# Who issues the bulk transfers of a pass: SP at its seventh place, or ScalarE at the end of its tenth

## The reference, cut to what matters

```python
xn = _layernorm(x, axis=-1)
x = x + _L0_gnn_ref(xn, edge_index, ...) + _L0_mix_ref(xn[None], ...)[0]
x = x + _L0_ffn_ref(_layernorm(x, axis=-1)[None], ...)[0]
...
# in _L0_ffn_ref
top_vals, top_idx = jax.lax.top_k(logits, K)          # K = 2 of E = 8
w = jax.nn.softmax(top_vals, axis=-1)
...
for e in range(E):
    h = jax.nn.gelu(jnp.einsum('bsd,dh->bsh', xn, W1[e]) + b1[e], approximate=False)
    y_e = jnp.einsum('bsh,hd->bsd', h, W2[e]) + b2[e]
    y = y + y_e * w_full[..., e, None]
```

## Time and profile before

| what | value |
|---|---|
| median of 3 runs | 3450.45 us (3449.42 to 3454.7) |
| the profiled execution's own time | 3450.09 us |
| its span, first to last instruction | 3448.4 us |
| PE busy | 2790.3 us, 81% of the span |
| DVE busy | 2317.2 us, 67% |
| POOL busy | 2153.7 us, 62% |
| ACT busy | 1283.3 us, 37% |
| the stage of the change | from about 2262 us to the end |

### The profile page before, as it was taken

The page is one execution under the profiler, slowest core; times in us unless marked ns, Lnnn a source line. Parts: engine busy times, 40 slices in busy tenths (PEclk is TensorE's granted clock), DMA queues, the critical chain, the costliest instruction groups (busy, mean ns, idle before and its releaser), DMA issues. The chain is left out here.

```text
span 3448.4 us, 69443 instructions
## 1 busy us (share of the span) xinstructions
PE 2790.3 (81%) x17326; PEld 2273.5 (66%) x17327; DVE 2317.2 (67%) x6448; ACT 1283.3 (37%) x4258; POOL 2153.7 (62%) x2115
## 2 busy tenths in 40 slices
PE   6858888888899988888888888845348798999998
PEld 4635666666676765666666666635247787999997
DVE  6656666666666666777777777788887676555554
ACT  5713333333333333333333333345445552333332
POOL 3167777777777777666676666705656576444444
PEclk9979999999999999999999999965569899999999
DMA  7646666666666657666666566646667776444443
GB/s 255 247 122 155 159 156 161 158 161 162 162 163 162 164 153 187 180 180 179 179 181 175 168 173 172 166 127 206 222 198 193 219 196 152 73 69 72 71 71 53
DMA packets 400457, 552.06 MB, mean 160 GB/s; under 512 B 64948, under 2 KB 332935, under 8 KB 399994
## 3 DMA queue, kind: packets, MB, share of 16 engines
q0 software_dynamic: 114496, 265.49, 32.9%
q1 hardware_dynamic: 200888, 205.86, 20.4%
q10 hardware_dynamic: 84770, 77.19, 7.0%
HBM read 416.82 MB, written 132.72 MB: 159 GB/s over the span
## 5 line engine op out<-in xcount | busy, mean ns | idle before, releaser
L1142 POOL DMA_INDIRECT rows<-node_rows,index x1552 | 1477.3, 952 | 562.3 <-issue 452.2
L1420 PE MATMUL ps_sum<-msg,hot 128*128 128x260 f32 x3904 | 1014.9, 405 | 18.9 <-DVE big L1239 2.9
L1420 PEld LDWEIGHTS ps_sum<-msg,hot 128*128 128x128 f32 x3904 | 726.7, 196 | 134.4 <-issue 7.7
L1222 DVE TENSOR_TENSOR msg<-rows,ps_w 128x1024 f32<-128x1024 f32 x488 | 595.8, 1221 | 37.2 <-ACT ps_w L1314 21.7
L1926 POOL DMA_INDIRECT out_dram<-big x204 | 359.6, 1763 | 358.2 <-DVE big L2192 261.6
L2066 PEld LDWEIGHTS x_ps_hT<-wq,x_w_ring 128*128 128x128 f32 x3264 | 403.3, 195 | 40.4 <-DVE x_w_ring L2159 24.0
L1986 ACT ACTIVATE wq<-x_ps_hT,x_b1T 128x128 f32<-128x128 f32 x816 | 232.9, 368 | 527.3 <-PE x_ps_hT L2066 527.2
L2066 PE MATMUL x_ps_hT<-wq,x_w_ring 128*128 128x128 f32 x3264 | 406.4, 279 | 26.5 <-DVE x_w_ring L2159 21.7
L1198 DVE TENSOR_SCALAR hotT<-targets,pair_node_id 128x512 bf16 x488 | 189.5, 388 | 348.3 <-SPq L1104 345.9
L1400 PE MATMUL ps_hot<-ident_h,hotT 128*128 128x128 bf16 x1952 | 194.2, 223 | 263.4 <-DVE hotT L1198 260.6
L1915 POOL DMA_INDIRECT expert_in<-f_rows,f_slot x196 | 251.4, 1283 | 206.5 <-DVE f_rows L2326 136.5
(11 more groups left out here) (304 smaller groups left out, 4302.8 us busy)
## 6 DMA issues: line engine op xcount, KB each, us to landing
targets<-dst_row SPq DMA_DIRECT2D x391, 128.0 KB
big<-expert_in SPq DMA_DIRECT2D x204, 130.0 KB, 2.1
rows<-node_rows,index POOLq DMA_INDIRECT x1564
x_w_ring<-in_L_ffn_W_dram SPq DMA_DIRECT2D x42, 512.0 KB, 5.1
node_rows<-big SPq DMA_DIRECT2D x14, 924.0 KB
turned<-rT SPq DMA_DIRECT2D x14, 896.0 KB, 4.6
area<-turned ACTq DMA_DIRECT2D x98, 128.0 KB
queries<-area ACTq DMA_DIRECT2D x98, 128.0 KB
```

Source lines behind the costliest of these rows:

```text
L1142: g.indirect_dma_start(rows[:, j, k, :], None, s.node_rows, bass.IndirectOffsetOnAxis(ap=index[:, b, j * G + k:j * G + k + 1], axis=0)).th ...
L1222: v.tensor_tensor(m[:, :, 0:D].rearrange("p g (h f) -> p g h f", h=GH), rows[:, bass.ds(here, 1), :, 0:D].rearrange("p j g (h f) -> p (j g ...
L1420: mm = pe.matmul(ps_sum[:, j % 2, 0:SUM], hot[:, j % MSGS, k * P:(k + 1) * P], msg[:, j % MSGS, k, :], start=(k == 0), stop=(k == G - 1))
```

## The change

The part at SP's place 7 is taken out, and the same four calls, with the same waits and transfers, stand in ACT's stream after all else that ACT has at place 10. `load_xn` and `load_hx` also stay on SP for the chunks loaded ahead of the rounds. Everything else is unchanged.

```diff
@@ SP @@
                         for it in TILES_AT[n, p]:
                             ahead(it)
-                        if p == 7 and n <= CHUNKS + 1:
-                            if n >= 2:
-                                settle_homes(n - 1)
-                            if n <= CHUNKS:
-                                store(n - 1)
-                            if n < CHUNKS:
-                                load_hx(n)
-                            if n + 1 < CHUNKS:
-                                load_xn(n + 1)
                         if p == 10 and n <= 3:
@@ ACT @@
+                def load_xn(c):
+                    if c >= 2:
+                        act.wait_ge(joined, c - 1)
+                    act.dma_start(xn[:, c % 2, :, :], s.residual[...]).then_inc(xn_loaded[c % 2], 16)
...
+                def settle_homes(freed):
...
+                    act.wait_ge(stored, 16 * freed)
+                    act.wait_ge(measured, freed)
+                    act.wait_ge(rows_ready, freed * CHUNK)
...
                         if p == 10 and 2 <= n < CHUNKS + 2:
                             odds_of(n - 2)
                         first_tiles([look_up, gelu], [0, 2], n, p)
+                        if p == 10 and 1 <= n <= CHUNKS + 1:
+                            if n >= 2:
+                                settle_homes(n - 1)
+                            if n <= CHUNKS:
+                                store(n - 1)
+                            if n < CHUNKS:
+                                load_hx(n)
+                            if n + 1 < CHUNKS:
+                                load_xn(n + 1)
```

More of the change, by code:

```diff
@@ L1762, in load_hx @@
                         sp.dma_start(x_row[0:TAIL, CHUNK - 1, :], x[N - TAIL:N, :]).then_inc(last_loaded, 16)
[L1764 to L1768, removed]
                 def load_fold(e):
@@ L1773, in load_fold @@
                     sp.dma_start(w_ring[:, e % 2, 0:C * HID].rearrange("p (c n) -> p c n", c=C), W1[e].rearrange("(c p) n -> p c n", p=P)).then_inc(fold_in[e % 2], 16)
[L1775 to L1786, removed]
                 def quad_expert_now(q):
@@ L1988, in gelu, with load_hx, store @@
                     ins.then_inc(act_ready, 1)
+                def load_xn(c):
+                    if c >= 2:
+                        act.wait_ge(joined, c - 1)
+                    act.dma_start(xn[:, c % 2, :, :], s.residual[c * CHUNK * P:(c + 1) * CHUNK * P, :].rearrange("(t p) d -> p t d", p=P))\
+                      .then_inc(xn_loaded[c % 2], 16)
+                def load_hx(c):
+                    full = min((c + 1) * CHUNK, TILES - 1) - c * CHUNK
+                    if c >= 1:
+                        act.wait_ge(joined, c)
+                    act.dma_start(hh[:, :, :], s.mixed[c * CHUNK * P:(c + 1) * CHUNK * P, :].rearrange("(t p) d -> p t d", p=P)).then_inc(hx_loaded, 16)
+                    act.dma_start(x_row[:, 0:full, :], x[c * CHUNK * P:(c * CHUNK + full) * P, :].rearrange("(t p) d -> p t d", p=P)).then_inc(hx_loaded, 16)
+                    if c == CHUNKS - 1:
+                        act.dma_start(x_row[0:TAIL, CHUNK - 1, :], x[N - TAIL:N, :]).then_inc(last_loaded, 16)
+                def store(c):
+                    full = min((c + 1) * CHUNK, TILES - 1)
+                    act.wait_ge(joined, c + 1)
+                    act.dma_start(out[c * CHUNK * P:full * P, :].rearrange("(t p) d -> p t d", p=P),
+                                 s.sums[:, c * CHUNK:full, 0:D]).then_inc(stored, 16)
+                def settle_homes(freed):
+                    homes_now = [e for e in range(EXPERTS) if -(-(RINGS + (e + 1) * W_HOME) // (CHUNK * ROW)) == freed]
+                    if freed != -(-RINGS // (CHUNK * ROW)) and not homes_now:
+                        return
+                    act.wait_ge(stored, 16 * freed)
+                    act.wait_ge(measured, freed)
+                    act.wait_ge(rows_ready, freed * CHUNK)
+                    if not homes_now:
+                        act.dma_start(b2_b.rearrange("p e d -> p (e d)"), b2.rearrange("e d -> (e d)").partition_broadcast(P)).then_inc(b2_in, 16)
+                    for e in homes_now:
+                        act.dma_start(w1[:, e, :].rearrange("p (c n) -> p c n", c=C), W1[e].rearrange("(c p) n -> p c n", p=P)).then_inc(experts_in, 16)
+                        act.dma_start(w2[:, e, :].rearrange("p (c n) -> p c n", c=HC), W2[e].rearrange("(c p) n -> p c n", p=P)).then_inc(experts_in, 16)
                 act.wait_ge(mix_root_in, 1)
```

## The result

The changed kernel takes 3544.35 us (median of 4, 3537.88 to 3555.36) against 3450.86 us for the kernel before on the same chip: ratio 1.0272, 95% interval 1.0245 to 1.0300. It is slower, as forecast, and the time lies in the range; it is 11 us above the forecast of 3533.

The account below looks back on a forecast made before the run. It took the pass as bound by the loop from `joined` through the burst to DVE's wait for `f_xn`, delays passing one for one into PE's full tail. 3450.09 + 54.2 (early rounds) + 28.8 (rounds 9 to 13) = 3533 us, range 3488 to 3565.

Parts of the forecast that it names:

- ACT's stream is held by an unmet wait: At the end of ACT's place 10, transfers cannot pass an activation still waiting; issue in round 7 is 6.52 us later.
- the rival built on it: Transfers overtake ACT's waiting activations and go out at `joined`; no early loss, 3423 to 3437 us, chance 0.04.
- 6.52 us per early round: Issue in rounds 2 to 7 comes 6.52 us later each, with nothing hiding it: 39.1 us.
- The shifts: Later issue alone in the early rounds: 39.1 us for rounds 2 to 7 and 3.5 for round 1, 42.6 together.
- The homes with the burst: Rounds 5 to 7: biases and experts' weights start together with the burst, 2.9 us each, 8.7 in all.
- `load_fold` beside the burst: Rounds 2 and 3: SP's load_fold runs beside the burst, 0 to 2.9 us each; half taken, 2.9.
- `xn(9)` hidden with 0.8 us to spare: Issued in round 8: 24.5 us to landing against DVE's use 25.3 us after `joined`, so no cost.
- Rounds 9 to 13: Late rounds, gelu also ahead of the transfers: 20.8 us for later issue plus 8 for sharing, 28.8, bounds 9.5 to 47.6.
- The first step: Round 9: the transfers stand behind the gelu, so `xn(10)` lands late; 12.6 to 15.1 us of new wait on DVE.
- my two bounds: Late rounds: issue when the gelu's product is there, 2.3 us before the odds start, or after the gelu, 2.7 after.
- The sharing with tile loads: Rounds 10 to 13: tile loads run beside the burst, up to 3.9 us each; half taken, 8 us.
- the rival of the longer hold: Issuing holds ACT more than about 13 us, delaying its rows to PE in four rounds; 3567 us, chance 0.09.

Follow-up runs that it names:

- e4: Changed kernel with the four calls at the head of ACT's place 10 instead of its end; 3459.05 us, ratio 1.0014 to the kernel before.
- e8: Changed kernel with settle_homes (biases, experts' weights) left on SP at place 7; 3521.54 us, ratio 1.0203 to the kernel before.
- e9: Changed kernel with load_fold issued by ACT behind load_xn instead of by SP; 3545.24 us, ratio 1.0265 to the kernel before.
- e3: Kernel before with SP waiting for gap_ready ahead of its four calls at place 7 from round 2 on; 3502.64 us, ratio 1.0141.
- e1: Changed kernel with ACT issuing the four calls only in rounds 1 to 8, SP at place 7 after that; 3516.30 us, ratio 1.0176 to the kernel before.
- e7: Kernel before with 14 idle activations more at the end of ACT's place 10 in rounds 10 to 13; 3457.56 us, ratio 1.0016.
- e6: Changed kernel with the calls on ACT in the order load_xn, load_hx, settle_homes, store; 3441.95 us, ratio 0.9972 to the kernel before.
- e5: Kernel before with SP's calls at place 7 in the order load_xn, load_hx, settle_homes, store; 3434.64 us, ratio 0.9948.
- e12: Kernel before with load_xn, then load_hx at SP's place 7, and settle_homes and store at SP's place 10; 3427.00 us, ratio 0.9912.

## Why the prediction was right, step by step

- **ACT's stream is held by an unmet wait** (from the earlier trace rows): right. In every round from 2 on the first transfer leaves with the odds or after them, never at `joined`. This is the step on which the sign hung. The rule of the Trainium skill, page "Advanced Engine Details and Errata", section "Sequencer and Instruction Queues", agrees with this trace only for activations that carry no wait (e4, eight passed); the rival built on it, 3423 to 3437, is out.
- **6.52 us per early round**: right, 6.56 in round 7. The shifts alone were set at 42.6 us (39.1 and 3.5 for round 1); taking the 11.3 that e8 shows for the homes, the 7.2 that e9 shows for `load_fold` and the 0.8 of `xn(9)` (below) from the 59.5 leaves 40.2. A burst with nothing beside it took 13.6 us from odds to L2221 (2416.99 to 2430.63, rounds 4 to 5), a little less than the 15.1 of the earlier trace rows.
- **The homes with the burst**: too small, 8.7 taken, 11.3 measured in the rounds 5 to 7 (e8). The bursts with them take 17.5 to 19.0 us, 3.4 to 4.1 more than the same bursts in e8, where 1.05 MB at 363 GB/s gave 2.9. The rate was taken too high: 363 GB/s is all that moved in the 3 us of the earlier trace rows, and 0.17 of those 1.09 MB were POOL's, which leaves about 306 GB/s for the burst. From issue to use, start included, its own 3.67 MB took 13.6 to 15.1 us, 244 to 269 GB/s. By these paces an estimate for 1.05 MB is 3.4 to 4.3 us.
- **`load_fold` beside the burst**: too small, and outside its own bounds of 0 to 5.8. 2.9 taken, 7.2 measured, 3.6 in each of the two bursts (e9). It needs both the second queue and the later burst: with the later burst in SP's one queue the two take 15.1 and 13.8 us (e3) instead of 18.5 and 17.3, and with ACT's queue on time nothing is lost (e4). Halving what could mix in was the larger error, the rate of 363 GB/s the smaller.
- **`xn(9)` hidden with 0.8 us to spare**: missed by as little; L2221 waited 0.85 us there.
- **Rounds 9 to 13**: 28.8 set, 33.2 measured up to the last join. The first step was 12.1 us (12.6 to 15.1 set). The issue fell 1.6 us behind the start of the odds (2880.43 against 2878.82, and alike in rounds 10 to 12), between my two bounds. It comes 0.08 us behind the start of the gelu's first activation (2880.35), with the load of the gelu's table ahead of that. The product that this gelu waits for was there by 2876.50, so the lower bound, an issue as soon as the product is there, was wrong. Whether the table or the gelu's own wait, long met, holds the transfer is not separated by any run.
- **The sharing with tile loads**: 8 set. From the first issue to the use it takes 20.6, 23.4, 19.3 and 21.6 us in rounds 10 to 13, against 18.8, 17.2 and 18.9 in rounds 10, 12 and 13 before (round 11's is taken against round 10's): 1.8 + 4.6 + 2.1 + 2.7 = 11.2. It lies midway between the half that I took and the 15.6 of everything mixed in. I read it as sharing. e4, which has the tile loads in the other queue too, takes 20.0 to 24.7 us in these rounds, and e1, e3 and e7, with the late burst in SP's queue, 17.1 to 21.1 in the rounds 10, 12 and 13. But the same round differs by one to three us among runs that issue it alike, and no run took the tile loads alone out, so sharing as the cause is argued and not shown.
- **PE**: the wait for expert rows nearly vanished, as forecast. What took its place are ACT's rows and not DVE's copies. That this had no price of its own up to 8.85 us of hold is shown by e7; the rival of the longer hold put that point at 13 us, and ACT was held for 10.0 to 13.6, so in round 13 that point was reached, and its price there is open.
- **The sum**: 54.2 + 28.8 = 83 set, 59.5 + 33.2 - 0.7 = 92 measured. The mechanism and its places held. Early, the homes (+2.6), `load_fold` (+4.3) and `xn(9)` (+0.8) came out above their terms and the shifts (-2.4) below; late, the longer burst came out above. That errors of both signs partly cancelled in the early sum is luck, though a small one.

What the prediction did not see is why a late issue costs at all. It took `f_xn` at the end of the burst as given; e6 shows that with `f_xn` in front the same late issue costs 7 to 14 us against e5 instead of 92, and that the kernel is then even faster than the one before.

## What to carry to other kernels

A transfer issued by a computing engine leaves when that engine's stream reaches it: look for the last activation ahead of it that waits for a semaphore, and put the issue ahead of that one or leave it to an engine whose stream has no such wait there. An engine that only issues can be late as well, as SP is behind the tile loads. Before moving a burst, look at its order: what is waited for goes first, what nobody waits for (a store) last. Here that alone turned 2.7% slower into 0.3% faster (e6), and on SP, with the store and the homes three places later, it made the kernel 0.9% faster than before (e12). And a wait that grows on an engine off the path, 8 to 41 us on PE in e7, is no loss until the time says so.

## What was not expected of the hardware

- How far ACT's stream runs ahead: a transfer went out past eight activations that carry no wait, 3.6 us before the last of them started (e4), but in the late rounds it came only with the start of the gelu, behind the load of its table and 1.6 us behind the odds.
- In these rows issuing held the engine longer when more was queued: the `f_x_row` issue took 1.4 us in round 2 of the changed kernel, 3.5 us in round 7 with weights ahead of it and 8.2 us in round 13 beside tile loads, and ACT did nothing else in that time.
- A transfer of another queue beside the burst cost about what its bytes cost at the burst's own pace: 1.05 MB of `load_fold` lengthened it by 3.6 us (e9), where the estimate above gives 3.4 to 4.3. At the 363 GB/s of the earlier trace rows it would have been 2.9.
